# The last two pairs of a fused cross-attention kernel: another order, other PSUM banks, shorter moment steps

## What is computed

```
layer 0: p2r = softmax(q(rgb) k(geo)^T * 16^-0.5) applied to v(geo), projected;  r2p the same with the roles swapped
         a   = rgb + p2r + geo + r2p
layer 1: attn = softmax((Wq y + bq)(Wk y + bk)^T / sqrt(128)) over the channels of a head, y = a
         o    = Wo (attn (Wv a + bv)) + bo + a
         out  = (o - mean(o)) * rsqrt(var(o) + 1e-5) * gn_w + gn_b      (mean and var over all of a batch)
```

## Time and profile before

| | us |
|---|---|
| median of three runs | 336.96 (336.56 to 337.16) |
| the profiled execution's own time | 336.94 |
| its span, first to last instruction | 335.2 |
| mean granted PE clock, share of full speed | 0.982 |
| PE, DVE, ACT, POOL busy | 313.4, 263.8, 231.2, 190.4 |

### The profile page before, as it was taken

How to read it: one execution, slowest core, us unless ns; L and a number is a source line. 1 busy time by engine, 2 the same in 40 slices (tenths; PEclk the granted TensorE clock), 3 DMA queues, 4 the chain that set the end, 5 groups by cost and what they waited for, 6 DMA issues and landing times.

```text
span 335.2 us, 12612 instructions
## 1 busy us (share of the span) xinstructions
PE 313.4 (94%) x4808; PEld 273.0 (81%) x4808; DVE 263.8 (79%) x716; ACT 231.2 (69%) x382; POOL 190.4 (57%) x277
## 2 busy tenths in 40 slices
PE   6999999999978999999999999999999999994980
PEld 3887898989866898988888898989898888972760
DVE  1595888988985788888898889888888999653574
ACT  3653757878785787878787797878787878954332
POOL 0874482757676275767667575757676675754010
PEclk9999999999999999999999999999999999997897
DMA  7999989498989949797998989797979670300215
GB/s 224 389 258 300 261 230 245 162 276 225 284 230 299 232 123 285 226 297 214 305 244 251 283 210 319 195 298 217 287 221 299 174 250 1 125 0 22 105 47 204
DMA packets 39061, 73.88 MB, mean 220 GB/s; under 512 B 4608, under 2 KB 26368, under 8 KB 39040
## 3 DMA queue, kind: packets, MB, share of 16 engines
q1 hardware_dynamic: 35008, 58.92, 64.6%
q10 hardware_dynamic: 4032, 14.68, 12.2%
HBM read 56.81 MB, written 16.78 MB: 220 GB/s over the span
## 4 chain that ended last, share of the span: by engine, by line
PE 88%; issue 3%; DVE 2%; POOL 2%; DMA 2%; ACT 2%; SPq 0%; POOLq 0%; ACTq 0%
PE oacc L429 10%; PE oacc L436 9%; PE oacc L430 9%; PE mid L526 5%; PE mid L454 4%; PE gacc L391 4%; PE mid L503 4%; PE stat L393 4%; PE tpx L348 4%; PE gacc L392 3%; PE gacc L393 3%; PE stat L392 3%; PE stat L391 3%; PE mid L512 2%; PE gacc L409 2%
## 5 line engine op out<-in xcount | busy, mean ns | idle before, releaser
L1129 POOL TENSOR_TENSOR xy_lo<-raw,xy_hi 128x256 fp32r<-128x256 f32 x256 | 179.9, 740 | 116.5 <-ACT xy_hi L696 116.5
L696 ACT ACTIVATE xy_hi<-raw 128x1024 fp32r<-128x1024 f32 x64 | 66.9, 1048 | 0.0
L856 DVE STREAM_TRANSPOSE t<-y_blocks 128x512 f32<-128x512 f32 x56 | 62.9, 1162 | 0.0
L429 PE MATMUL oacc<-xy_hi,pq_hi 128*128 128x512 f32 x124 | 55.6, 448 | 5.0 <-ACT res L703 4.8
L885 DVE BATCH_NORM_STATS2 hstat<-res 128x6 f32<-128x512 f32 x60 | 40.1, 688 | 22.8 <-ACT res L703 22.7
L703 ACT ACTIVATE res<-oacc 128x512 f32<-128x512 f32 x60 | 35.6, 594 | 30.7 <-PE oacc L436 30.4
L430 PE MATMUL oacc<-xy_lo,pq_hi 128*128 128x512 f32 x124 | 50.0, 403 | 1.5 <-issue 1.5
L394 PE MATMUL gacc<-t 128*32 128x225 f32 x224 | 45.4, 354 | 0.0
L393 PE MATMUL gacc<-t 128*32 128x225 f32 x224 | 45.4, 354 | 0.0
L394 PE MATMUL stat<-t 128*32 128x225 f32 x224 | 44.9, 353 | 0.0
L393 PE MATMUL stat<-t 128*32 128x225 f32 x224 | 44.9, 353 | 0.0
(11 more groups left out here) (146 smaller groups left out, 916.8 us busy)
## 6 DMA issues: line engine op xcount, KB each, us to landing
raw<-in_x SPq DMA_DIRECT2D x31, 512.0 KB, 5.7
raw<-in_ctx SPq DMA_DIRECT2D x31, 512.0 KB, 7.0
y_blocks<-in_ctx SPq DMA_DIRECT2D x112, 128.0 KB, 7.0
out<-res ACTq DMA_DIRECT2D x28, 512.0 KB, 3.4
x_blocks<-in_x SPq DMA_DIRECT2D x56, 128.0 KB, 6.7
out<-res SPq DMA_DIRECT2D x4, 512.0 KB, 2.8
wt<-in_weights SPq DMA_DIRECT2D x1, 896.0 KB, 7.0
raw<-in_x SPq DMA_DIRECT2D x2, 256.0 KB, 3.7
```

The costliest lines, as they stand in the source:

```text
L429: pe.matmul(bank[:, :], whi, xy_hi[slot][:, s, cols], start=(s == 0), stop=False)
L696: act.activation(xy_hi[slot][:, s, :], raw[slot][:, s, :], ACT.Copy).then_inc(split_hi, 1)
L856: dve.transpose(dst, blocks[:, HC * i:HC * (i + 1)]).then_inc(yt_ready, 1)
L1129: piece = pool.tensor_tensor(xy_lo[slot][:, s, cols], raw[slot][:, s, cols], xy_hi[slot][:, s, cols].bitcast(f32), ALU.subtract)
```

## The change

The u12, u3, score and probability tiles of pair 15 move to `tpx[0]` and `tpx[1]`, which hold nothing after the last transposition. With that, u12 and u3 of pair 15 go ahead of `pq_products(14)`. The order of steps 16 and 17 is rewritten on PE, ACT and DVE, `pq_products(15)` moves from step 17 into step 16, and the outputs of batches 29, 30 and 31 go to other banks. On ACT, `norm_scale(13)` and what follows it go behind all copies of pair 14. Batch 27's `normalise` stays in step 16, batch 29's goes from DVE to ACT, as does `norm_scale` of batch 30. Of nine `keep_warm` matmuls one stays. POOL's program is unchanged. In `partition_moments` and `variance`, which all pairs use, intermediate tiles go, and per-batch fused instructions take the place of some.

```diff
+        tail = [tpx[i].rearrange("p m r -> p (m r)") for i in range(2)]
+        u12_bank, u3_bank = (mid0, tail[0]), (mid1, tail[1])
+        sc = [bank[:, k:k + 6 * W32].rearrange("p (i c) -> p i c", c=W32) for bank, k in ((mid0, 0), (tail[1], 2 * C))]
+        probs = [bank[:, k:k + 6 * W32].rearrange("p (i c) -> p i c", c=W32) for bank, k in ((mid0, 6 * W32), (tail[0], 0))]
+        abv_s = [bank[:, 12 * W32:12 * W32 + 2] for bank in (mid0, tail[0])]
-        o_last = [oacc, [gacc, mid1]]
+        o_next = [oacc, [gacc, oacc[0]]]
+        o_last = [tail, [oacc[1], gacc]]
@@ PE, step 16
-                    pq_products(p - 2)
-                    u12_products(p - 1)
-                    group_moments(p - 3)
-                    u3_products(p - 1)
-                    out_half(h - 1, u, 0, 0)
-                    scores(p - 1)
-                    out_half(h - 1, u, 0, 1)
-                    out_half(h - 1, u, 1, 0)
-                    out_half(h - 1, u, 1, 1)
-                    z_operands(p - 1)
+                    u12_products(p - 1, True)
+                    u3_products(p - 1, True)
+                    pq_products(p - 2)
+                    scores(p - 1, True)
+                    out_half(h - 1, u, 0, 0, parts=(0,))
+                    out_half(h - 1, u, 0, 1, parts=(0,))
+                    out_half(h - 1, u, 0, 0, parts=(1,))
+                    out_half(h - 1, u, 0, 1, parts=(1,))
+                    z_operands(p - 1, True)
                     keep_warm(1)
                     z_products(p - 1)
-                    keep_warm(4)
+                    out_half(h - 1, u, 1, 0, banks=o_next, bank_free=0)
+                    group_moments(p - 3)
                     m_products(p - 1, True)
-                    keep_warm(2)
+                    out_half(h - 1, u, 1, 1, parts=(0,), banks=o_next, bank_free=2 * n + 3)
+                    pq_products(p - 1)
+                    out_half(h - 1, u, 1, 1, parts=(1,), banks=o_next)
@@ PE, step 17: pq_products(p - 2) and keep_warm(2) go; each half 1 is cut in two parts, group_moments between them
@@ ACT, step 16
+                    u12_out(p - 1, True)
+                    keys_times_sums(p - 1)
                     pq_high(p - 2, u)
-                    u12_out(p - 1)
-                    keys_times_sums(p - 1)
                     split_high(h - 1, 1, 1, 0, True)
+                    exponent(p - 1, True)
                     split_high(h - 1, 1, 1, 1, True)
+                    out_to_sbuf(h - 1, u, 0, 0)
+                    out_to_sbuf(h - 1, u, 0, 1)
+                    z_out_last(p - 1)
+                    out_to_sbuf(h - 1, u, 1, 0, o_next)
+                    pq_high(p - 1, 1 - u)
+                    out_to_sbuf(h - 1, u, 1, 1, o_next)
                     norm_scale(p - 3)
-                    out_to_sbuf(h - 1, u, 0, 0)
                     normalise(*before(h, u), 0)
-                    exponent(p - 1)
-                    out_to_sbuf(h - 1, u, 0, 1)
+                    store(*before(h, u), 0)
                     normalise(*before(h, u), 1)
-                    store(*before(h, u), 0)
-                    out_to_sbuf(h - 1, u, 1, 0)
                     store(*before(h, u), 1)
-                    out_to_sbuf(h - 1, u, 1, 1)
-                    z_out_last(p - 1)
@@ ACT, step 17
-                    pq_high(p - 2, u)
-                    norm_scale(p - 3)
+                    norm_scale(p - 3)
                     normalise(h - 1, 0, 0)
+                    normalise(h - 1, 0, 1)
+                    norm_scale(p - 2, slice(0, 1))
                     normalise_last(h - 1, u, 0, range(2))
                     normalise_last(h - 1, u, 1, range(1))
@@ DVE, partition_moments and variance (all pairs)
-                dve.tensor_tensor(mean_s[:, bs], pstat[:, bs, 0], cshift[u][:, bs], ALU.add)
                 dve.tensor_tensor(mom[:, 0, bs], pstat[:, bs, 0], cshift[u][:, bs], ALU.add).then_inc(mean_ready, 1)
                 dve.wait_ge(mean_ready, count)
-                dve.tensor_tensor(square[:, bs], mean_s[:, bs], mom[:, 0, bs], ALU.mult).then_inc(square_ready, 1)
-                dve.wait_ge(square_ready, count)
-                dve.tensor_tensor(mom[:, 1, bs], pstat[:, bs, 1], square[:, bs], ALU.add).then_inc(mom_ready, 1)
+                for b in range(bs.start, bs.stop):
+                    mean = mom[:, 0, b:b + 1]
+                    last = dve.scalar_tensor_tensor(out=mom[:, 1, b:b + 1], in0=mean, scalar=mean,
+                                                    in1=pstat[:, b, 1:2], op0=ALU.mult, op1=ALU.add)
+                last.then_inc(mom_ready, 1)
...
-                dve.tensor_tensor(gsquare[:, bs], stat_mb[:, 0, bs], gmean[:, bs], ALU.mult).then_inc(gsquare_ready, 1)
+                for b in range(bs.start, bs.stop):
+                    last = dve.scalar_tensor_tensor(out=gsquare[:, b:b + 1], in0=stat_mb[:, 0, b:b + 1],
+                                                    scalar=gmean[:, b:b + 1], in1=eps, op0=ALU.mult, op1=ALU.subtract)
+                last.then_inc(gsquare_ready, 1)
                 dve.wait_ge(gsquare_ready, count)
-                dve.scalar_tensor_tensor(out=gvar[:, bs], in0=stat_mb[:, 1, bs], scalar=EPS, in1=gsquare[:, bs],
-                                         op0=ALU.add, op1=ALU.subtract).then_inc(gvar_ready, 1)
-                dve.wait_ge(gvar_ready, count)
-                dve.tensor_scalar(var[:, bs], gvar[:, bs], EPS, None, ALU.max).then_inc(var_ready, 1)
+                for b in range(bs.start, bs.stop):
+                    last = dve.scalar_tensor_tensor(out=var[:, b:b + 1], in0=stat_mb[:, 1, b:b + 1],
+                                                    scalar=gsquare[:, b:b + 1], in1=eps, op0=ALU.subtract, op1=ALU.max)
+                last.then_inc(var_ready, 1)
@@ DVE, step 16
                     half_stats(*before(h, u), 1, 1)
+                    u3_out(p - 1, True)
                     half_moments(p - 3)
+                    shift_scores(p - 1, True)
+                    pq_low(p - 2, u)
+                    softmax_out(p - 1, True)
                     partition_moments(p - 3, 1 - u)
-                    pq_low(p - 2, u)
-                    variance(p - 3, 1 - u)
-                    u3_out(p - 1)
                     half_stats(h - 1, u, 0, 0)
-                    shift_scores(p - 1)
-                    softmax_out(p - 1)
+                    z_out_last(p - 1)
                     half_stats(h - 1, u, 0, 1)
-                    z_out_last(p - 1)
-                    half_stats(h - 1, u, 1, 0)
                     n12_out(p - 1)
                     n3_out(p - 1)
+                    variance(p - 3, 1 - u)
                     c_out(p - 1, 1 - u)
+                    half_stats(h - 1, u, 1, 0)
+                    pq_low(p - 1, 1 - u)
                     half_stats(h - 1, u, 1, 1)
@@ DVE, step 17: pq_low(p - 2), normalise and norm_scale_last(p - 2, 0) go; half_stats_last(0, 0) goes ahead of variance(p - 3)
```

More of the change, by code:

```diff
@@ L312, in _ @@
             refill_raw(last - 1, 1, 1)
[L313 to L316, removed]
+            store(last + 1, 0, 0)
+            store(last + 1, 0, 1)
+            store(last + 1, 1, 0)
+            store(last + 1, 1, 1)
             for n in range(4):
@@ L330, in keep_warm @@
                 for k in range(count):
-                    pe.matmul(tpx[0][:, 0, :], warm[:, 0:C], warm[:, C:2 * C], start=True, stop=True)
+                    pe.matmul(gacc[:, 0:C], warm[:, 0:C], warm[:, C:2 * C], start=True, stop=True)
             pe.wait_ge(warm_set, 1)
@@ L411, in gram_full_width, with out_half @@
                     mm.then_inc(gram_done, 1)
-            def out_half(h, u, b, half, last=False, parts=range(2)):
-                bank = o_last[b][half] if last else oacc[half]
+            def out_half(h, u, b, half, parts=range(2), banks=(oacc, oacc), bank_free=None):
+                bank = banks[b][half]
                 slot = 2 * u + b
@@ L424, in out_half @@
                         pe.wait_ge(split_lo, 2 * n + 2)
-                    if not (last and b == 1):
+                    if bank_free is None:
                         pe.wait_ge(o_out, 2 * n + 1 + half)
+                    elif bank_free:
+                        pe.wait_ge(o_out, bank_free)
                     for s in range(2):
@@ L449, in u12_products, with u3_products, scores @@
                 pe.wait_ge(gram_ready, 2 * p + 2)
-                if not (isinstance(p, int) and p < 1):
+                if last:
+                    pe.wait_ge(xt_ready[0], 2 * PAIRS)
+                elif not (isinstance(p, int) and p < 1):
                     pe.wait_ge(c_ready, p)
                 for a in range(2):
-                    dst = mid0[:, a * 2 * C:(a + 1) * 2 * C]
+                    dst = u12_bank[last][:, a * 2 * C:(a + 1) * 2 * C]
                     mm = pe.matmul(dst, gram[:, a, XC:GW], wt[:, 0:2, :], start=True, stop=True)
                 mm.then_inc(u12_done, 1)
```

(30 more changed lines are left out.)

84 lines of the change are left out of this document (35 added, 49 removed).

## The result

| | us |
|---|---|
| the changed kernel, median of four executions | 327.46 (326.61 to 329.37) |
| the kernel before beside it | 336.76 (336.05 to 337.16) |
| ratio, 95% interval | 0.9734 (0.9684 to 0.9784) |
| the profiled execution, its span | 328.15, 326.3 |

Forecast was 324.5, range 323.0 to 327.6. The ratio on the 336.96 of the table before makes 328.0: the direction and most of the size are right, and the time lies above the range, by 0.4 us. The median alone, 327.46, is just inside it. In three later sets the ratio was 0.9686 (0.9635 to 0.9737), 0.9696 (0.9628 to 0.9764) and 0.9617 (0.9562 to 0.9671). Some executions of each kernel took several us longer than the rest, and all comparisons leave these out.

What follows compares the result with a forecast made beforehand. PE was taken as the loop's bound, with looseness in the last 40 us. The tail's end at 322.8 instead of 335.2 gave 12.4 us; loop moments and fillers gave nothing: 336.94 less 12.4 is 324.5, range 323.0 to 327.6.

Steps and rivals of the forecast that it cites:

- The step that failed: End of PE's step 15: taken as 294.92 us in both kernels, the start for laying out the new order.
- The tail's gain: Steps 16 and 17 to the span's end: end at 322.8 against 335.2, 12.4 us less.
- the tail's unknowns: Forecast's own range, 323.2 to 325.7: below without ACT's 0.7 and the store's 0.3, above with store's 0.9 and late hand-overs.
- the slower case: Loop, 14 pairs: new moments later than PE's 1.97 us slack; 1.1 us more per pair gives 338.3; chance 0.02.
- The bias term: ACT's queue of put-off work near the end: `norm_scale` of batch 30 done at 316.9.
- the last variance waits for ACT and not for moments: DVE, batch 31: `variance` waits for ACT until 316.9, though its moments are there at 316.2.
- the end hangs on this wait: Kernel's end: ACT sets it by 0.7 us, through the last variance's wait for batch 30's `norm_scale`.
- The clock: Rival, new tail: PE's clock falls in step 16, some 3 us of path work doubles, 327.5 us; chance 0.10.
- DVE's queue: Rival, step 16: three or four hand-overs late by 0.4 us each make 1.5, 326.0 us; chance 0.13.
- The stall: Rival, step 16: PE keeps its 4.8 us wait and half clock, gain about 6 us, 331 us; chance 0.03.

Runs made afterwards that it cites:

- b3: Changed kernel with the last variance no longer waiting for ACT's bias of batch 30: ratio 0.9643 to the kernel before, tail 28.28 us.
- d1: Kernel before with the second loads of batches 4 to 7 cut to their first 512 columns: 337.36 us.
- b4: Kernel before with, in ACT's step 16, pair 14's copies, the exponent and the z copies moved ahead of `norm_scale(13)`, normalisations and stores: ratio 0.9827.
- c2: Kernel before with 38 filler matmuls put ahead of batch 29's products in PE's step 16: ratio 1.0044 to the kernel before.
- a4: Changed kernel with the old moments and variance functions, so the new order alone: ratio 0.9684 to the kernel before.
- a3: Kernel before with only the new moments and variance functions, in the old order: ratio 1.002 to the kernel before.
- b1: Changed kernel run a third time, no edit: early standstills 3.85 + 0.77 us, tail 28.2 us; no time or ratio given under this label.
- d3: Changed kernel run a fourth time, no edit: 325.48 us, ratio 0.9617 to the kernel before.
- c3: Changed kernel with ten warm-up matmuls at PE's start instead of two: ratio 0.9815 to the kernel before.
- c1: Changed kernel with the second loads of batches 4 to 7 cut to their first 512 columns: 325.51 us, ratio 0.9678 to the kernel before.
- c4: Changed kernel with the last variance's wait moved and 96 already-met waits ahead of PE's first matmul: four times, 324.61 to 333.02 us.
- d2: Changed kernel with the second loads of batches 4 to 7 cut to their first 512 columns, run again: 323.98 us.

## Why the prediction was wrong, point by point

**The step that failed** is the first of the sum, "I lay the new order out from 294.92, where PE finishes step 15 in both kernels". It was 298.08 in the first profile, 298.3, 299.6 and 293.7 in the next three. The tail's gain was subtracted from one execution, and the range was made of the tail's unknowns alone; that all that stands before it repeats was taken for granted. What does not repeat are PE's early standstills: sums of 4.2, 2.5, 4.6 and 0 us in four profiles of the changed kernel, 0.33 in the one I read of the kernel before. They make the shift. At the same matmul ahead of the first place the changed kernel was 0.3 us early (40.41 against 40.71), behind the second it was 3.9 us late (50.33 against 46.44), and over the loop that shrank to 3.16, in small steps whose cause no run sought. The list of waits held two rows of `issue`, of 1.8 and 1.5 us, that I passed over. Read, their sum as an estimate would have put some 3 us on either side of the forecast, and the four sets lie within that: ratios between 0.9617 and 0.9734 are 324.1 to 328.0 us of 336.96. One number of the rivals was wrong as well and changed nothing: 14 times 1.1 us on 324.5 is 339.9, not the 338.3 of the slower case.

**The tail** was forecast as 27.9 us (294.92 to 322.8) and is 28.2 in every profile of the changed kernel. Set beside the measured rows with 3.16 us added:

| | forecast + 3.16 | measured |
|---|---|---|
| scores on PE | 300.4 | 300.38 |
| z | 304.7 | 304.72 |
| m | 307.2 | 307.17 |
| pq(15) | 309.6 | 309.72 |
| batch 30's products | 311.5 | 311.46 |
| `norm_scale(13)` | 311.9 | 311.78 |
| bias of batch 30 ready | 320.1 | 320.42 |
| last output | 321.7 | 322.16 |
| from there to the end | 4.3 | 4.1 |

The bias term was 0.36 us short, part of it a POOL power that ACT met 0.48 us late at 316.21, where I had only ACT's own queue. That the last variance waits for ACT and not for moments is shown by DVE's 0.68 us wait. That the end hangs on this wait, as the prediction had it, is not so: b3 takes it away and the end stays, since the two stores lie behind it.

**Where the gain comes from.** The tail before, 40.3 us in the first profile, is 39.5 in d1: the half clock ended sooner there. Of 11.3 to 12.1 us, moving the copies gives 6.4 to 7.2 (b4), of which the half clock that follows the standstill is at most 2.1 to 2.8 (c2); moments under 0.1 to 0.5 (a4, a3). The rest, 4.9 us from b4's tail to the changed kernel's less what the moments give, is the order and the banks together, and I did not part these two: in the changed kernel pair 15's scores are done before pair 14's products, and its z, m and n have these products beside them. That this is how the rest is gained is read from the rows and not tested.

**The rivals.** The clock did not fall without the fillers, 1.00 until the last products. DVE's queue did not bound step 16: no PE wait over 0.22 us up to batch 30. The stall did not stay. The loop did not slow down: a3 is equal to before.

**What the standstills are.** At the first place PE, its weight loads and nothing else stop for 2.6 us while the DMA engines' share is 1.03. In the 8 us around it (38 to 46 us, changed kernel) the DMA queues are:

```profile
q1 hardware_dynamic: 1118, 2.12, 102.0%
q8 instruction: 1, 0.02, 0.8%
```

One block of instructions goes through in that time, beside the loads. Between 125 and 290 us, where the loop goes round, there is one such block and no standstill. The trace's record of single transfers says when each block moved (q8; all are 16384 bytes; us):

| profile, place | block moves | PE stops | PE goes on |
|---|---|---|---|
| changed kernel, first | 41.21 to 42.30 | 41.26 | 43.87 |
| b1, first | 43.77 to 44.88 | 42.46 | 46.31 |
| changed kernel, 1336th matmul | 101.69 to 103.01 | 102.56 | 104.27 |
| d3, first | 40.51 to 41.61 | does not | 42.96 |
| c3, first | 37.24 to 38.56 | does not | 44.18 |

All 17 profiles have 52 standstills by `issue` of over 0.25 us that lie behind 20 us, and in each of the 52 PE goes on 1.2 to 1.6 us after such a block has landed. That shows what PE waits for: its own code. Two of 0.41 us near 19.7 us (b4, c1) have no block near them. The transfer itself takes 0.9 to 1.5 us in the 52, whether loads fill the engines or not (1.09 us in the first row, beside a share of 1.03; 1.32 in the third, between 101.70 and 103.00, beside 0.18); it is its start that comes early or late.

The Trainium skill, "Runtime: NRT & Kernel Launch", section "Instruction fetch mechanics", says that an engine's code is streamed in 16 KiB blocks by a DMA queue of its own while the block before runs, that crossing to the next is mostly hidden, and that a taken branch to a block not held forces a fetch. The size agrees with the trace; "mostly hidden" does not hold here, with up to 3.85 us at a time. That the loop's pair of standstills belongs to code is shown by the blocks and by its moving with the code ahead of it (c3, c4); that it is the branch is only argued. The early pair is gone in the three runs that start later, which all have more code ahead too; in c3 the block was there 5.6 us before PE came to its place. That the loads are why a block starts late fits c1, d1 and d2, with sums of 0.83, 1.11 and 0.56 us, but 0 and 0.33 occur with whole loads too, so this stays likely and not shown. The length in one execution is how late the block starts; what decides that is open.

## What to carry to other kernels

Look for the instruction that frees a buffer and ask what stands ahead of it in its engine's queue: here a 0.5 us copy stood behind a power that nothing needed yet, and one move of lines gave more than half of a large rebuild's gain. A long wait of PE costs its own length and can cost a half clock behind it, here 4.8 and up to 2.8 us. Before a difference is laid on one profiled execution, take the rows of `issue` in it as a term with a range of its own. A fixed point late in the kernel, from which the changed part is measured, tells a gain of 11 us to under 1 us (28.2 in four profiles of the changed kernel, 39.5 to 40.3 in three with the old tail and moments), where the sets of medians spread over 4.

## What I had not expected of the hardware

- PE waits for its own code, up to 3.85 us at a time and 7.8 us in sum in one execution of the changed kernel (b1), whose span is 327.8 us.
- 96 waits that are already met held PE until 6.64 us, against 1.46 us without them, 54 ns each; 24 matmuls of two columns at the start took 7.14 us, 0.30 us each. While these ran, with PE busy throughout, its clock fell to half, as the last row shows, in the columns of the earlier trace rows:

```profile
6.64 2.90 PE L322 MATMUL oacc<-warm 128*128 128x384 f32 x4 [6.64 <-issue]
```

```profile
4.18 7.14 PE L332 MATMUL oacc<-warm 128*128 128x2 f32 x48
```

```profile
8.20:11.10 2.90, 2.90 (x15) 2.90 (x16) 0.00 (x0) 0.00 (x0) 0.00 (x0) 0.50 1.01 391
```
